# Preparing 256 tokens before a selective scan, and the other seven units of 256 inside it

## What is computed

```python
x0 = n(x)                                             # layer norm without weights
xn = (x0 - mean) / sqrt(var + 1e-5) * norm_w + norm_b # a second one, with weights
delta, B, C = split(xn @ x_proj_w.T, [128, 192])
dt = softplus(delta @ dt_proj_w.T + dt_proj_b)
C = C[:, arange(L) % 64, :]                           # only C of the first 64 tokens is used
A = -exp(A_log)                                       # (256, 64)
h = exp(dt[:, :, None] * A) * h + dt[:, :, None] * B[:, None, :] * xn[:, :, None]   # token by token
y = einsum('bdn,bn->bd', h, C)
x = x + (y + x0 * D_param) @ out_proj_w.T             # x0 * D_param: the skip term
x = x + moe(n(x)); x = x + attention(n(x)); x = x + ffn(n(x))
```

## Time and profile before

| | us |
|---|---|
| median of 3 runs | 1304.5 |
| lowest and highest run | 1299.48, 1305.68 |
| span of the profiled execution | 1301.5 |

### The profile page before, as it was taken

One profiled execution on the slowest core, in us unless ns is written; L12 is line 12 of the kernel. 1 busy time (PEld: TensorE's weight loads), 2 busy tenths in 40 slices (PEclk: granted clock), 3 DMA queues, 4 the chain that ended last, 5 costly groups with the idle time before them and its releaser, 6 DMA issues.

```text
span 1301.5 us, 29730 instructions
## 1 busy us (share of the span) xinstructions
PE 1102.2 (85%) x12064; PEld 704.2 (54%) x12064; DVE 820.0 (63%) x999; ACT 508.0 (39%) x1253; POOL 308.2 (24%) x930
## 2 busy tenths in 40 slices
PE   3637888889888888888884899999999598999998
PEld 2525444444544454444442677888887255475565
DVE  5858999999999999999995121111111566342111
ACT  3865555566555665566652111111111111212110
POOL 9741222222233222432244011111111200000000
PEclk9765899898899999998997899999999798999999
DMA  3798345443223222322214922232200400000000
GB/s 108 237 279 229 79 101 129 128 112 93 55 45 93 60 54 50 87 53 51 51 53 189 326 77 97 101 102 101 80 17 13 133 1 1 1 9 8 17 17 17
DMA packets 171833, 112.31 MB, mean 86 GB/s; under 512 B 93653, under 2 KB 162264, under 8 KB 169392
## 3 DMA queue, kind: packets, MB, share of 16 engines
q1 hardware_dynamic: 163264, 88.95, 24.4%
q0 software_dynamic: 8000, 20.87, 4.9%
q10 hardware_dynamic: 432, 0.59, 0.2%
HBM read 63.44 MB, written 45.90 MB: 84 GB/s over the span
## 4 chain that ended last, share of the span: by engine, by line
PE 49%; DVE 26%; issue 14%; SPq 5%; ACT 4%; DMA 2%; POOL 1%; DVEq 0%; ACTq 0%; POOLq 0%
DVE h L1159 20%; PE psum L1410 11%; PE psum L1422 11%; PE psum L1922 8%; PE psum L1933 4%; PE psum L943 2%; PE psum L1865 2%; ACT decay L1044 2%; PE psum L929 2%; PE psum L910 1%; SPq L199 1%; SPq L278 1%; PE psum L1857 1%; PE psum L1909 1%; SPq L282 1%
## 5 line engine op out<-in xcount | busy, mean ns | idle before, releaser
L1159 DVE TENSOR_TENSOR_SCAN h<-decay,psum 128x1024 f32<-128x1024 f32 x256 | 565.0, 2266 | 13.3 <-ACT psum L1054 7.8
L1044 ACT ACTIVATE decay<-psum 128x512 f32<-128x512 f32 x512 | 279.2, 600 | 195.9 <-PE psum L910 190.6
L929 PE MATMUL psum<-xdiag,bstat 96*128 96x64 bf16 x4096 | 175.6, 199 | 58.1 <-DVE h L1159 55.5
L929 PEld LDWEIGHTS psum<-xdiag,bstat 96*128 96x128 bf16 x4096 | 144.2, 102 | 84.5 <-DVE h L1159 77.2
L910 PEld LDWEIGHTS psum<-rows,shared 32*128 32x128 bf16 x4096 | 78.5, 96 | 181.7 <-issue 116.6
L943 PE MATMUL psum<-h,cstat 128*32 128x512 f32 x1024 | 149.0, 659 | 1.5 <-DVE h L1159 1.5
L1410 PE MATMUL psum<-xdt,shared 128*128 128x320 f32 x512 | 141.9, 439 | 0.7 <-ACT xdt L1469 0.7
L1422 PE MATMUL psum<-shared,hid 128*128 128x256 f32 x640 | 139.5, 379 | 0.6 <-ACT hid L1463 0.6
L1315 POOL TENSOR_TENSOR carry<-decay,h 128x16 f32<-128x16 f32 x240 | 58.2, 242 | 340.9 <-ACT decay L1044 340.6
L1422 PEld LDWEIGHTS psum<-shared,hid 128*128 128x128 f32 x640 | 121.0, 190 | 17.2 <-issue 1.1
L910 PE MATMUL psum<-rows,shared 32*128 32x64 bf16 x4096 | 109.9, 195 | 14.9 <-ACT decay L1044 7.6
(11 more groups left out here) (205 smaller groups left out, 1083.5 us busy)
## 6 DMA issues: line engine op xcount, KB each, us to landing
shared<-in_w SPq DMA_DIRECT2D x16, 1024.0 KB, 4.8
xdiag<-x_parts_d SPq DMA_DIRECT2D x256, 48.0 KB
x_parts_d<-x_parts POOLq DMA_DIRECT2D x46, 256.0 KB, 7.7
parts_d<-dt_parts SPq DMA_DIRECT2D x24, 256.0 KB, 8.6
rows<-parts_d SPq DMA_DIRECT2D x128, 48.0 KB
disp_d<-zero SPq DMA_DIRECT2D x4, 1305.0 KB, 8.2
xd<-disp_d SPq DMA_DIRECT2D x8, 652.5 KB, 6.2
picked_d<-zero SPq DMA_DIRECT2D x4, 1024.0 KB, 5.2
```

Source lines behind the costliest of these rows:

```text
L929: ins = pe.q.matmul(to.rearrange("p d (s e) -> p s d e", e=2), bstat[0:ROWS, c % 2, b, :], xdiag[0:ROWS, c % 2, b, :, d, :], start=True, s ...
L1044: act.q.activation(decay[:, gi % NB, 8 * half:8 * half + 8, :], per_d(bank_a[half]), ACT.Exp).then_inc(sem("exp"), 1)
L1159: dve.q.tensor_tensor_scan(out=h[:, half_slot(c, half), ch:ch + G, :].rearrange("p d t -> p (d t)"), data0=decay[:, gi % NB, :, :].rearran ...
```

## The change

Tokens are prepared in eight units of 256. `prologue`, in place of `prepare`, takes unit 0 alone, and the statistics of all tokens (`rstd`, `mean_neg`). The other seven become steps of the schedule (`unit_steps`), 19 for each unit, at most one a group, those that open bank_z only at the groups that `opens` names. What VectorE did for them is done by GpSimd (sums, products and subtractions, from SBUF) and ScalarE (relu, and copies out of PSUM for GpSimd); TensorE turns and projects. All stores, the loads of astat among them, are on SyncE's queue; where n parts are alike, one DMA writes them from a broadcast source. The x loads of a chunk are 4 in place of 8. The skip term is no longer stored: GpSimd scales x from `xres` (`skip_in`), and TensorE adds it in `yT` by products with the identity that accumulate in the same bank. `HS` is 4, the y steps, keep-awake groups and places of the zero fills are moved, `r_xt` has two slots, and the scalar engine's table is set to the one with exp and ln after each square root.

The core of the diff:

```diff
-DECAY_PAIRS = ((0, 0), (1, 0), (2, 0), (0, 1), (1, 1), (0, 2))
+DECAY_PAIRS = ((0, 0), (0, 1), (0, 2), (1, 0), (1, 1), (2, 0))
...
+MOVED = ((0, 3), (3, 2), (5, 1))
...
+LOADS = ((("dt", 0), ("dt", 1), ("dt", 2), ("dt", 3), ("b", 0), ("b", 1)), (("x", 0), ("x", 1)), (("x", 2), ("x", 3)))
...
+            sp.q.dma_start(xa[:, early, :], x_in[:, early, :]).then_inc(sem("x_ld_early"), 16)
+            sp.q.dma_start(ident[:, :], a["c_ident"]).then_inc(sem("consts"), 16)
+            sp.q.dma_start(s["cols"][:, :, :], a["cols"]).then_inc(sem("consts"), 16)
+            sp.wait_ge(sem("w_first"), 48)
+            for t in (slice(UT, TILES // 2), slice(TILES // 2, TILES)):
+                sp.q.dma_start(xa[:, t, :], x_in[:, t, :]).then_inc(sem("x_ld_late"), 16)
+            sp.wait_ge(sem("a_lo"), 1)
+            sp.q.dma_start(s["decay_parts_d"].rearrange("j h p m -> p j h m"), a_parts[:, :, :, :]).then_inc(sem("a_parts_st"), 16)
+            sp.wait_ge(sem("a_parts_st"), 16)
+            for g in range(ROWG):
+                for m, n in MOVED:
+                    row = 32 * g + DH * m
+                    sp.q.dma_start(s["astat"][row:row + DH * n, RCH * g:RCH * (g + 1), :],
+                                   s["decay_parts_d"][0:n, :, RCH * g:RCH * (g + 1), :].rearrange("j h q m -> (j h) q m")
+                                   ).then_inc(sem("astat_ld"), 16)
+            sp.wait_ge(sem("u_dthi"), 1)
+            store_dt(k, s, 0, 0)
+            sp.wait_ge(sem("x_hi"), 1)
+            store_x(k, s, 0, 0)
+            sp.wait_ge(sem("u_blo"), 1)
+            for j in range(3):
+                store_b(k, s, 0, j)
+            sp.wait_ge(sem("u_dtmid"), 1)
+            store_dt(k, s, 0, 1)
+            sp.wait_ge(sem("u_xmid"), 1)
+            store_x(k, s, 0, 1)
+            sp.wait_ge(sem("u_dtlo"), 1)
+            store_dt(k, s, 0, 2)
+            sp.wait_ge(sem("u_xlo"), 1)
+            store_x(k, s, 0, 2)
+            sp.wait_ge(sem("bstat_zero"), 1)
+            sp.wait_ge(sem("xdiag_zero0"), 1)
+            sp.wait_ge(sem("st_dt"), DT_ST)
+            sp.wait_ge(sem("st_b"), B_ST)
+            load_rows(k, s, 0, LOADS[0])
+            sp.wait_ge(sem("st_x"), X_ST)
+            load_rows(k, s, 0, LOADS[1] + LOADS[2])
+            sp.wait_ge(sem("xdiag_zero1"), 1)
+            load_rows(k, s, 1, sum(LOADS, ()))
 
         def on_pool():
+            pool.q.memset(a_parts[:, :, :, :].bitcast(F32), 0.0).then_inc(sem("a_zero"), 1)
+            pool.q.memset(s["x_parts"][:, :, :].bitcast(F32), 0.0).then_inc(sem("words_zero"), 1)
...
+            both_sd(0, early)
+            act.q.preload_act_table_set("natural_log_exp_and_others")
...
+            both_sd(1, late)
+            act.q.preload_act_table_set("natural_log_exp_and_others")
...
+            dve.wait_ge(sem("x_ld_late"), 32)
+            moments(range(UT, 6))
             dve.wait_ge(sem("a_mid"), 1)
             dve.wait_ge(sem("a_rest"), 1)
+            dve.q.tensor_tensor(a_part[2], a_rest[:, :, :], a_part[1], ALU.subtract).then_inc(sem("a_lo"), 1)
...
-HS = 5
+HS = 4
...
-Y_STEPS = ((0,), (), (1,), (), (2,), (), (3,))
+Y_STEPS = ((0,), (1,), (), (2,), (), (3,))
+AWAKE = (2, 3, 6, 0)
...
+def unit_steps(u):
+
+    yield ([("u_load",)] if u == 1 else []) + [("u_norm",)]
+    yield [("u_turn",)]
+    yield [("u_xn",)]
+    yield [("u_proj",)]
+    yield [("u_take",)]
+    yield [("u_dt",), ("u_brest",)]
+    yield [("u_abs",), ("u_bmid",)]
+    yield [("u_relu",), ("u_blo",)]
+    yield [("u_soft",)]
+    yield [("u_sum",)]
+    yield [("u_dthi",), ("u_dtx",)]
+    yield [("u_tx",), ("u_dtrest",), ("u_store_dt", 0), ("u_store_b", 0)]
+    yield [("u_xhi",)]
+    yield [("u_dtmid",), ("u_store_x", 0)]
+    yield [("u_dtlo",), ("u_store_dt", 1), ("u_store_b", 1)]
+    yield [("u_xrest",), ("u_store_b", 2)]
+    yield [("u_xmid",), ("u_store_dt", 2)]
+    yield [("u_xlo",), ("u_store_x", 1)] + ([("u_load_next",)] if u + 1 < UNITS else [])
+    yield [("u_store_x", 2)]
...
+    opens = lambda c, j: j in ((1, 3, 5) if c < 3 else (1, 3) if c % 2 else (4, 6))
...
+        yield from advance(units, c, j)
+        yield from advance(routing, c, j)
...
+                elif kind in ("u_load", "u_load_next"):
+                    u = x[0] + (kind == "u_load_next")
+                    sp.wait_ge(sem("st_dt"), DT_ST * u)
+                    sp.q.dma_start(ux[:, :, :], x_in[:, UT * u:UT * (u + 1), :]).then_inc(sem("u_ld"), 16)
...
-                if j % 2 and gi > GROUPS * CPB // 4 + 1:
+                if j in AWAKE and gi > GROUPS * CPB // 4 + 1:
...
+                    pe.wait_ge(sem("xs"), c + 1)
                     for th in range(CT):
+                        for dh in range(DH):
+                            pe.q.matmul(turned_in(th)[:, :, dh, :], xs[:, dh * P:(dh + 1) * P],
+                                        ident[:, T * th:T * (th + 1)].rearrange("p (q j) -> p q j", j=16), start=dh == 0, stop=False)
...
-                            ins = pe.q.transpose(to, y_sb[:, th, :], ident[:, :])
+                            ins = pe.q.matmul(to, y_sb[:, th, :], ident[:, :], start=False, stop=True)
...
+                elif kind == "u_proj":
+                    u, z = x
+                    pe.wait_ge(sem("z_free"), z)
+                    for dh in range(DH):
+                        ins = pe.q.matmul(half_z(0), s["w_proj"][:, dh, 0:RANK], uxn[:, dh, :], start=dh == 0, stop=dh == 1)
+                    for i in range(UT):
+                        for dh in range(DH):
+                            ins = pe.q.matmul(by_tile[:, i, :], uxn[:, dh, P * i:P * (i + 1)],
+                                              s["w_proj"][:, dh, RANK:RANK + STATE], start=dh == 0, stop=dh == 1)
+                    if u == UNITS // BATCH:
+                        ins = project_c(pe, s, bank_z[:, 384:384 + CSPAN])
+                    ins.then_inc(sem("u_proj"), 1)
...
+                elif kind == "u_take":
+                    u, z = x
+                    act.wait_ge(sem("u_proj"), u)
+                    act.wait_ge(sem("u_dtrest"), u)
+                    act.wait_ge(sem("st_b"), B_ST * u)
+                    act.q.copy(s["delta"], half_z(0))
+                    act.q.copy(s["b_f"], by_tile)
+                    if u == UNITS // BATCH:
+                        act.q.copy(s["cmat"][:, 1, :], bank_z[:, 384:384 + CSPAN]).then_inc(sem("c_taken"), 1)
...
+                elif kind == "u_soft":
+                    u = x[0]
+                    act.wait_ge(sem("u_abs"), 2 * u)
+                    act.q.activation(s["e_all"], s["e_all"], ACT.Exp, scale=-1.0).then_inc(sem("u_exp"), 1)
+                    act.wait_ge(sem("u_exp"), u)
+                    act.q.activation(s["e_all"], s["e_all"], ACT.Ln, bias=s["one"][:, 0:1]).then_inc(sem("u_ln"), 1)
...
+                elif kind == "u_xhi":
+                    u, z = x
+                    act.wait_ge(sem("u_px"), u + 1)
+                    act.wait_ge(sem("st_x"), X_ST * u)
+                    act.q.copy(s["x_f"], tx)
+                    act.q.copy(x_part[0], tx).then_inc(sem("z_free"), 1)
...
-                    if x[0] == len(ROUTED) - 1:
-                        act.q.activation(warm[:, :], eps[:, 0:1], ACT.Exp)
+                    act.q.preload_act_table_set("natural_log_exp_and_others")
...
-                    dve.wait_ge(sem("y"), c - 2 + half)
+                    dve.wait_ge(sem("y"), c - 1)
...
+                elif kind == "skip_in":
+                    i = x[0]
+                    pool.wait_ge(sem(f"xres_ld{i % 2}"), 16 * (i // 2 + 1))
+                    pool.wait_ge(sem("yT"), i)
+                    pool.wait_ge(sem("skip_row"), 16)
+                    pool.q.tensor_scalar(xs[:, :], xres[:, i % 2, :], mean_neg[:, i:i + 1], s["rstd"][:, 0, i:i + 1], ALU.add, ALU.mult
+                                         ).then_inc(sem("xs_normed"), 1)
+                    pool.wait_ge(sem("xs_normed"), i + 1)
+                    pool.q.tensor_tensor(xs[:, :], xs[:, :], drow[:, :], ALU.mult).then_inc(sem("xs"), 1)
+                elif kind == "u_norm":
+                    u = x[0]
+                    pool.wait_ge(sem("u_ld"), 16 * u)
+                    for n in range(UT):
+                        i = UT * u + n
+                        ins = pool.q.tensor_scalar(ux[:, n, :], ux[:, n, :], mean_neg[:, i:i + 1], s["rstd"][:, 1, i:i + 1],
+                                                   ALU.add, ALU.mult)
...
+                elif kind == "u_sum":
+                    u = x[0]
+                    pool.wait_ge(sem("u_ln"), u + 1)
+                    pool.wait_ge(sem("z_free"), relu_at[u])
+                    pool.q.tensor_tensor(s["e_all"], s["e_all"], s["r_all"], ALU.add).then_inc(sem("u_dt"), 1)
```

855 lines of the change are left out of this document (404 added, 451 removed).

## The result

The changed kernel takes 1369.5 us (median of four runs, 1352.8 to 1383.8) against 1304.8 for the kernel before: ratio 1.045, 95% interval 1.0415 to 1.0487. So it is slower, by 65 us, where I gave 0.82 to faster.

What follows compares the result with a forecast made beforehand. VectorE was taken to bound the scan, with 1.1 us of room a chunk. 1301.5 - 57 (preparation) + 6 (start) + 18 (units) - 3 (clock) + 1 (tail) = 1266.5 us of span; forecast 1269, range 1243 to 1300.

Steps and rivals of the forecast that it cites:

- the clock: TensorE in the scan: few idle gaps, so fewer half-clock stretches, taking back 3 of 7.8 us (7 back to 8 lost).
- The price of a half-clock stage: Scan: were the granted clock near 0.5 throughout, a group with y would take 3.8 us and the forecast be wrong.
- First scan: Preparation: first scan at 43 us (38 to 50) in place of 100.11, a gain of 57 us (50 to 62).
- rival (e): Preparation: first scan still after 65 us because SyncE's single queue holds it; 1291 us, chance 0.04.
- Start of the scan: First chunk: 4.3 us for GpSimd's wait on unit 1, 3 for half-clock TensorE, less 1.3; net +6 (2 to 14).
- Units and skip terms: Units 2 to 7 inside the scan: about 3 us late a unit, +18 us for six (0 to 36).
- the ring: Scan: TensorE's decays and ScalarE's exp wait on each other; 74.2 us per four chunks against VectorE's 71.4.
- Rival (a): Scan: it hides the units, two groups of lead are kept and excesses don't add; about 1252 us, chance 0.20.
- rival (b): Scan: TensorE-ScalarE loop fuller than counted, 6 us a unit in place of 3, 5 more at start; 1292 us, chance 0.14.
- Tail: After the last scan: GpSimd's sum goes, about 0.5 us of products come, a table load of 1.28 waits; +1 us.
- (c): Units in the scan: exp and ln tables reload, 2 x 1.28 us per unit, +18; about 1287 us, chance 0.04.
- (d): GpSimd's unit steps in the scan run slower than its 1.46 us a group; at 3.3 us each 1346 us, chance 0.13.

Runs made afterwards that it cites:

- a_in128: The changed kernel with only the input products on 128 rows in place of 96, zeros in the added rows: 1282.1 us, ratio 0.981.
- b_strip12: The kernel before with only the decay products' strips cut from 32 rows to 12: 1386.3 us, ratio 1.065.
- t_uload: The changed kernel with inputs on 128 rows and unit 1's x tiles loaded ahead of chunk 1's parts in SyncE's queue: 1271.5 us, ratio 0.978.
- i_nounits: The changed kernel with inputs on 128 rows and units 1 to 7 left out on every engine (later tokens wrong): 1259.1 us, ratio 0.964.
- i_early: The changed kernel with inputs on 128 rows and keep-awake products from the third group on, using the identity's words: 1282.3 us, ratio 0.983.
- t_skip: The changed kernel with inputs on 128 rows and the last tile's skip_in ahead of the last group's scatters on GpSimd: 1275.8 us, ratio 0.980.
- t_all: The changed kernel with inputs on 128 rows, the last skip_in ahead of the scatters, unit 1's early load and early keep-awake products: 1268.8 us, ratio 0.974.
- b_12_128: The kernel before with decay products on 12 rows in place of 32 and input products on 128 in place of 96: 1300.0 us, ratio 0.997.
- a_nounits: The changed kernel, inputs on 96 rows, without units 1 to 7; every chunk reads the first 256 tokens' parts: 1408.0 us, ratio 1.081.
- a_strip32: The changed kernel with decay products on strips of 32 rows again, 20 of them zeros cleared by GpSimd: 1295.5 us, ratio 0.991.
- s_tight: The changed kernel with 32-row decay strips and the cleared part of the decay weights cut to a quarter: 1291.9 us, ratio 0.987.

## Why the prediction was wrong, point by point

**The step that failed is the clock.** I put down -3 us, between 7 back and 8 lost, on the ground that "TensorE will have few idle gaps". With the clock kept up (a_in128) the stage is 615.4 us, with the changed kernel's clock 692.3: the term is +77. (At half clock the changed kernel's scans are some 3.3 us apart, at full clock 2.36; over some 95 scans of the half-clock time that makes an estimated 89 us, in line with it.) Two errors stand in it. First, I took gaps for what lowers the clock. The Trainium skill, TensorE: Matmul & The Clock Gate, Part 1, says that too, that the clock follows how busy TensorE has been lately. The runs here don't bear it out as the whole rule: TensorE is busy for 19.48 of 20 us at a granted clock of 0.50, and over the stage it is busier in b_strip12 (598.9 of 659.0 us, clock 0.73) than in the kernel before (494.9 of 589.4, clock 0.93), whose products it shares but for the rows; the measurements decide. Second, a part of the change had no term at all: the diff turns `slice(32 * g, 32 * (g + 1))` into `slice(32 * g, 32 * g + PAIR_ROWS)`, and the forms in the earlier trace rows say `32*128`. I read it as an edit that saves two clearings. The costs of an edit are not only the durations of its instructions: those of the decay products are the same (0.41 us for 16 at the full clock on 12 rows or 32). My bound of 8 us lost was worked out from no row, though one shows a whole window at 0.50. The price of a half-clock stage I did write down, at the end, at 3.8 us for a group with y. The stretch above has 4.28 us with a unit's turn of 1.10 in it, so without the turn 3.2: the price was of the right size, somewhat high, and it should have been a rival with a chance.

**First scan**: forecast 43 us (38 to 50), measured 40.20. SyncE's chain of issues was the bound, as reckoned (the input products wait for its load of xdiag until 39.03 us); rival (e) falls.

**Start of the scan**: forecast 4.3 us for u_load and 3 for the cold TensorE, less 1.3. The wait of GpSimd cost 5.5 (t_uload takes it away), and a_in128 has 2.2 us more behind input products.

**Units and skip terms**: forecast 18 us (0 to 36) at the full clock. With the clock kept, the stage is 26.0 us longer than before: 12.2 of that stay without units (i_nounits, which still makes the skip terms), 5.5 are u_load's wait, 8.3 the units' own. The forecast for the whole stage was +21. Each of these is a difference of single profiled runs, and the stage of nearly the same kernel was 620.2 (i_early) and 621.7 (t_skip) in others. So the ring was sized well to about 5 to 11 us. Rival (a), 18 us under the forecast, is off by 23; rival (b), 23 over it, is off by 18, or by 12 beside those two.

**Tail**: forecast +1, measured +6.9, and t_skip shows why. I costed "about 0.5 of new products" in place of a sum on GpSimd, and did not look at what is queued ahead of the new step on its engine: the scatters, one every 1.3 us. The lost 6 us, some of them the half clock behind the wait, are the mis-sized term that counts second.

**Rivals (c) and (d)** fall by these rows: GpSimd's 512-wide steps take 1.1 to 1.27 us as forecast, and there is no load of a table beside the router's. Of these I had said 3 or 4 in the scan and found 7, two for nearly every root of the router, as the kernel before has them too; (c) had 14 for the units.

```profile
L1393 POOL TENSOR_TENSOR ue<-ue,ur 128x512 f32<-128x512 f32 x7 | 8.9, 1271 | 0.3 <-issue 0.3
L1413 POOL TENSOR_TENSOR uxn<-ur,x_parts 128x512 f32<-128x512 f32 x7 | 8.9, 1265 | 0.0
L1418 POOL TENSOR_TENSOR x_parts<-uxn,x_parts 128x512 bf16<-128x512 f32 x7 | 7.7, 1097 | 0.0
...
L1153 ACT ACT_TABLE_LOAD x5 | 6.4, 1283 | 0.1
L1154 ACT ACT_TABLE_LOAD x5 | 6.4, 1283 | 0.1
```

**The sum again**, for a_in128's profiled run: 40.6 + 615.4 + 618.1 = 1274.2 us, against 43 + 610.4 + 613 = 1266.4. That is within 8 us for everything but the clock, but with some luck: it is the quickest of a_in128's four runs. By the ratio, 0.981, some 25 us are gained on the kernel before, where the forecast had 35. That t_all comes out at the forecast's 1269 is no merit of it: it is another kernel, with the clock, the tail and unit 1's load mended.

**What stays open.** What exactly the clock follows: the runs show that it depends on the rows that matmuls take, whatever these hold, and wide products of one kind make up for narrow ones of another, in one program on one core. A product and its weight load take the same rows, so which of the two counts can't be told; that the units' products help because they take all rows is argued. Why a spell, once begun, lasts up to 38 us in the changed kernel and mostly under 10 before stays open. The medians of the variants with 128 rows differ by less than their spreads in several pairs, and what is said of those rests on stages and tails of one profiled run each.

## What to carry to other kernels

When an edit narrows a matmul (fewer rows of the contraction, a slice cut to its data), compare the granted clock of the stage before and after, and not the durations at the full clock: here 20 rows of zeros a product were worth some 70 us, and 32 rows of zeros on other products some 85. Padding these contractions to 128 rows with zeros cost no TensorE time (0.64 us for 16 products on 96 rows and on 128) where the buffers were cleared anyway, and it is worth a run in a kernel whose clock dips while TensorE is busy. And of each step that moves to another engine, ask what stands ahead of it in that engine's queue at the one place where it ends the chain.

## What the runs showed of the hardware

- The granted clock of a stage went from 0.93 to 0.73, and the kernel from 1304.9 to 1386.3 us, when 16 of a group's matmuls took 12 rows in place of 32 (b_strip12), and back to 0.95 when 16 others took 128 in place of 96 (b_12_128), with all added rows zero.
- With inputs on 96 rows, taking out the units' products (all on 128 rows) lowered it from 0.77 to 0.63 (a_nounits); with inputs on 128 rows it stayed at 0.94 to 0.95 (i_nounits, a_in128).
- Two VectorE steps that take 0.74 us together took 8.75 beside GpSimd clearings of 6.92 and 1.95 us, and 3.63 beside clearings of 1.80 and 1.95 (a_strip32, s_tight): each step ended with a clearing.
- A TensorE-bound loop at half the clock stayed there for whole windows while busy: 19.48 us of 20 busy at 0.50.
- A profile's clock can read 1.00 where its records have not begun: the changed kernel's first 38 us of scan read as full clock, with every batch of 16 input products at 1.03 us, where the full clock gives 0.64.
